# Filling the fourth 32 rows of the score operands with zeros, so that the score matmuls contract over all 128 rows

## The chip, the cores and the metric

The kernel runs on one core of one Trainium2 chip. The metric is the device time of one execution in microseconds (us). Every time below is of that one core.

## The reference

One block of a perceiver: cross attention from 256 queries to a context of 25088 rows, self attention over the 256 rows, and a feed-forward net, each with a residual. The change touches only the cross attention, whose scores go through a sigmoid and not a softmax:

```python
E, H, D = 512, 16, 32
q = (layernorm(x) @ Wq.T).reshape(B, L, H, D) * D ** -0.5      # L = 256
k = (ctx @ Wk.T).reshape(B, -1, H, D)                          # 25088 rows
v = (ctx @ Wv.T).reshape(B, -1, H, D)
scores = sigmoid(einsum('blhd,bshd->bhls', q, k))
o = einsum('bhls,bshd->blhd', scores, v).reshape(B, L, E)
x = x + o @ Wo.T
x = x + self_attention(layernorm(x))
x = x + ffn(layernorm(x))                                      # hidden width 2048
```

## The kernel before

The context is worked through in 49 chunks of 512 rows. The first chunk, then 22 turns of a loop over two chunks (`odd`, then `even`), then four more chunks written out. Float32 products are made from rounded parts: each operand is split into a high part and a rest (type float32r), and three of the four products of parts are added (`TERMS`).

Keys (line 748) and values (line 773) of a chunk are each made by a scheme of seven products of half-size blocks, `keys(1)` to `keys(7)` and `values(1)` to `values(7)`. One such product is 12 matmuls over 128 rows with 256 columns each. The vector and scalar engines add the products up, and the keys' high part and rest are copied by DMA into the key stack `kst`: for each head the 32 rows of the high part go to rows 0 to 31 of the stack, the rest to rows 32 to 63, and the high part once more to rows 64 to 95. The query stack `qst` holds the high part of the queries in rows 0 to 31, the same high part in rows 32 to 63, and the rest in rows 64 to 95. So one matmul over 96 rows gives all three products of a head of 32. Rows 96 to 127 of both stacks are not used by the scores before the change.

A score unit (line 789) is four such matmuls, one for each head of a group of four heads, against 128 context rows. It is written into one of two score tiles `sc`, and ScalarE takes the sigmoid of the whole unit (line 376) into `probs`. A chunk has 16 units. The weighing with the values (line 809) has four matmuls per unit, each over 128 rows, which write 32 rows of the sum `acc` side by side.

The order of TensorE's work is written out by hand. Mostly a pair of units (8 matmuls) is followed by a key product (12) and a value product (12). An entry into scores is a place where TensorE comes to line 789 from another line. The functions of the order give 8 entries in the first chunk, 9 in each of the next 46 (`odd` or `even`), 13 in chunk 47 (with the pairs of chunk 48 that it does ahead) and 3 in chunk 48: 8 + 46 * 9 + 13 + 3 = 438 entries with 784 units in all. Of these, 7 per chunk in 48 chunks, 336, are followed at once by key matmuls.

Several tiles lie on the same memory at different times. The second half of `kst` (`spare`) first holds sums of weights (`wk_sum`) and the transposed input (`xnT`), which the weight rounding and the query projection (line 870, semaphore `q_made`) read. Small unused tiles (`gap`) shift the addresses of some of the operands.

Of the kernel before, what the change touches and what calls it, by code (L numbers as in the profile page):

```python
# [21 lines left out]
P = 128  # L22
# [4 lines left out]
D = E // H  # L27
# [16 lines left out]
def f32(ap):  # L44
    return ap.bitcast(F32)
# [60 lines left out]
def cross_attention(nc, x, ctxT, wqT, wkT, wvT, woT, wqk, wv, bv, wo, w_all, biases, keep):  # L106
# [4 lines left out]
    ident, x1, qst, next_weights = keep["ident"], keep["x1"], keep["rows"][0], keep["weights"][1]  # L111
    with ExitStack() as stack:
# [3 lines left out]
        def sem(name):  # L116
            return stack.enter_context(nc.semaphore(name))
# [15 lines left out]
        kst, kst_f32 = keep["two_types"](stack, "k_stack", [P, 2, 2, HG, 2, HS])  # L133
# [40 lines left out]
        ident_zero, const_ready, chain = sem("ident_zero"), sem("const_ready"), sem("dve_chain")  # L174
        var_ready, sd_ready, xn_ready = sem("var_ready"), sem("sd_ready"), sem("xn_ready")
        xnT_made, xnT_ready, q_made = sem("xnT_made"), sem("xnT_ready"), sem("q_made")
        one_ready, zeros_ready = sem("one_ready"), sem("zeros_ready")
        xn1_ready, xn1T_made, xn1T_ready = sem("xn1_ready"), sem("xn1T_made"), sem("xn1T_ready")
        bv_loaded, v1_made, v1_ready = sem("bv_loaded"), sem("v1_made"), sem("v1_ready")
        q_hi, q_lo, q_stacked = sem("q_hi"), sem("q_lo"), sem("q_stacked")  # L180
        wk_summed, wv_summed = sem("wk_summed"), sem("wv_summed")
        wk_hi, wv_hi, wk_ready, wv_ready = sem("wk_hi"), sem("wv_hi"), sem("wk_ready"), sem("wv_ready")
# [164 lines left out]
        @block.gpsimd  # L347
        def _(pool):
            nc.gpsimd.memset(keep["one"][:, 0:1], 1.0).then_inc(one_ready, 1)
            nc.gpsimd.memset(zeros[:], 0.0).then_inc(zeros_ready, 1)  # L350
            nc.gpsimd.memset(bits[:], 0).then_inc(piece_used, 1)
            nc.gpsimd.memset(ident[:], 0.0).then_inc(ident_zero, 1)
            pool.wait_ge(ident_zero, 1)
            nc.gpsimd.affine_select(out=ident[:], in_=ident[:], compare_op=ALU.not_equal, fill=1.0,
                                    base=0, pattern=[[-1, P]], channel_multiplier=1).then_inc(const_ready, 1)

        @block.scalar
        def _(act):
# [354 lines left out]
        def _(pe):  # L713
# [66 lines left out]
            def scores(c, n, order, free):  # L780
                t, g = order[n]
                if free:
                    pe.wait_ge(probs_ready, c * (TC * G) + (n - 1))
                if t % 2 == 0 and g % 2 == 0:
                    q = {(0, 0): 0, (0, 2): 1, (2, 2): 2, (2, 0): 3}[t, g]
                    pe.wait_ge(lo_moved[q], c * MOVED + MOVED)
                    pe.wait_ge(hi_twice[q], c * 16 + 16)
                for j in range(HG):
                    last = nc.tensor.matmul(sc[g % 2][:, j * L:(j + 1) * L],  # L789
                                            kst[0:3 * D, t // 2, g // 2, j, g % 2, t % 2 * P:(t % 2 + 1) * P],  # L790
                                            qst[0:3 * D, j, g, :], start=True, stop=True)
                last.then_inc(scores_ready, 1)

            def weigh(c, par, units, order, first=False):
# [81 lines left out]
            for ready in (wk_ready, wv_ready):  # L876
                pe.wait_ge(ready, 8)
            pe.wait_ge(q_stacked, 3 * MOVED)

            def one(c, par, first, k_next, split_next, looped):  # L880
                m = c + 1
# [3 lines left out]
                def unit(n):  # L885
                    scores(c, n, order, not (first and n < 2))
# [19 lines left out]
                def last_pair(p):  # L906

                    scores(m, 2 * p, order, True)
                    scores(m, 2 * p + 1, order, True)
# [141 lines left out]
            for a, to in enumerate((kp, vp)):  # L1051
                for n, g in enumerate(GROUPS_DONE):
                    if a == 1 and n == G - 1:
# [3 lines left out]
                                            start=n == 0, stop=n == G - 1)  # L1057
# [513 lines left out]
def build(nc, x, ctxT, wqT, wkT, wvT, woT, wqk, bqk, wv, bv, wn, bn, wo, bo,  # L1571
          w_all, s1, s2, sh1, sh2, s3, out):
    with ExitStack() as stack:
# [6 lines left out]
        def two_types(stack, name, shape):  # L1580

            with nc.sbuf_tensor(f"{name}_r", shape, F32R) as as_f32r:
# [14 lines left out]
        keep |= {"wn": sb("wn_sb", [P, KE, H]), "bqk": sb("bqk_sb", [P, 2 * KE]),  # L1597
                 "bn": sb("bn_sb", [H, 1]), "bias_loaded": sem("bias_ld")}
        cross_attention(nc, x, ctxT, wqT, wkT, wvT, woT, wqk, wv, bv, wo, w_all, (wn, bqk, bn), keep)
        keep |= {"any_inexact": sb("any_inexact", [1, 1], mybir.dt.int32), "inexact_ready": sem("any_inexact_ready"),  # L1600
                 "x2": sb("x2", [P, LT, E]), "raw": sb("w_raw", [P, RING, UNIT]),
# [53 lines left out]
```

## Time and profile before

| | |
|---|---|
| Time, median of 3 runs | 1924.5 us (1924.48 to 1924.76) |
| Span of the profiled execution | 1916.8 us |
| Outside the span, by the median | 7.7 us |
| PE busy | 1903.9 us, 99% |
| DVE, ACT busy | 1201.8 us, 1014.5 us |
| POOL busy | 4.3 us |
| Granted TensorE clock | 1.00 from the first stretch to the last |

The profile page gives no separate device time for the profiled execution, only its span. The time of the kernel is therefore compared as its median, and the 7.7 us between span and median are what lies around the span. PE stands for TensorE's matmuls, PEld for its weight loads, DVE for the vector engine, ACT for the scalar engine, POOL for GpSimd. A matmul's own duration overlaps that of the next; how fast they follow each other is read from the starts of two groups and the number of matmuls between them.

### The profile page before, as it was taken

The page shows a single profiled execution, that of the slowest core. Times are in us where ns is not written, and L with a number is a line of the kernel's source. Part 1 is how long each engine was busy: PE and PEld are TensorE (multiplying, and loading weights), DVE is VectorE, ACT ScalarE, POOL GpSimd, SP SyncE. Part 2 cuts the span into 40 slices and gives each one's busy share as a digit, 9 for nine tenths or more (in the row PEclk, how much of TensorE's full clock was granted, in tenths as well). Part 3 has the DMA queues.
Part 4 walks back from the last instruction along what each step waited for, and adds up shares of the span by engine and source line. Part 5 has one row for each costly group of instructions (what it writes and reads, how often), then busy time and mean ns, then how long its engine had stood idle before and what let it go on. Part 6 is the DMA issues. An engine that isn't in the chain of part 4 may idle for free. (4 is left out here: it accounts for less than half of the span.)

```text
span 1916.8 us, 50813 instructions
## 1 busy us (share of the span) xinstructions
PE 1903.9 (99%) x19361; PEld 1708.7 (89%) x19362; DVE 1201.8 (63%) x2113; ACT 1014.5 (53%) x1132; POOL 4.3 (0%) x16
## 2 busy tenths in 40 slices
PE   9999999999999999999999999999999999999999
PEld 7989999999898999999889999999989999867998
DVE  7566676667667576666766766676676775436322
ACT  5455455555544555455554555545455454634864
POOL 0000000000000000000000000000000000000000
PEclk9999999999999999999999999999999999999999
DMA  7556555565656656566565565656556555454784
GB/s 212 149 154 169 142 153 159 155 157 142 167 147 156 169 132 157 154 159 156 152 167 144 149 166 140 166 140 162 150 156 165 141 153 128 108 219 147 279 303 165
DMA packets 128396, 310.92 MB, mean 162 GB/s; under 512 B 33889, under 2 KB 33889, under 8 KB 109665
## 3 DMA queue, kind: packets, MB, share of 16 engines
q1 hardware_dynamic: 95952, 214.10, 43.7%
q10 hardware_dynamic: 32400, 96.22, 15.9%
q8 instruction: 30, 0.49, 0.1%
q14 instruction: 14, 0.11, 0.0%
HBM read 153.95 MB, written 0.52 MB: 81 GB/s over the span
## 5 line engine op out<-in xcount | busy, mean ns | idle before, releaser
L376 ACT ACTIVATE probs<-sc 128x1024 f32<-128x1024 f32 x784 | 769.8, 1025 | 730.6 <-PE sc L789 594.9
L748 PE MATMUL kp<-x_combos,weights_r 128*128 128x256 f32 x4032 | 536.0, 280 | 0.0
L748 PEld LDWEIGHTS kp<-x_combos,weights_r 128*128 128x128 f32 x4032 | 491.5, 188 | 28.7 <-issue 28.4
L773 PE MATMUL vp<-more_weights,x_combos 128*128 128x256 f32 x4032 | 515.7, 277 | 0.0
L773 PEld LDWEIGHTS vp<-more_weights,x_combos 128*128 128x128 f32 x4032 | 485.3, 188 | 0.6 <-issue 0.4
L789 PE MATMUL sc<-rows_r,k_stack_r 96*128 96x256 f32 x3136 | 436.6, 280 | 0.1
L789 PEld LDWEIGHTS sc<-rows_r,k_stack_r 96*128 96x128 f32 x3136 | 396.3, 189 | 2.8 <-issue 1.6
L583 DVE TENSOR_TENSOR parts<-parts,kp 128x512 f32<-128x512 f32 x240 | 164.4, 685 | 325.7 <-PE kp L748 325.7
L809 PE MATMUL acc<-probs,v 128*32 128x256 f32 x6272 | 354.4, 380 | 0.0
L809 PEld LDWEIGHTS acc<-probs,v 128*32 128x32 f32 x6272 | 196.4, 110 | 131.0
L520 DVE TENSOR_TENSOR x_combos<-ctx_raw,x_combos 128x512 fp32r<-128x512 f32 x240 | 166.2, 692 | 8.2
L608 DVE TENSOR_TENSOR v<-parts,vp 128x512 f32<-128x512 f32 x144 | 98.8, 686 | 60.9 <-PE vp L773 60.9
L614 DVE TENSOR_TENSOR bits<-bits,weights 128x512 int32<-128x512 int32 x176 | 121.3, 689 | 24.1 <-DMA weights<-w_all_dram 20.2
L533 DVE CAST x_combos<-ctx_raw 128x512 fp32r<-128x512 f32 x240 | 101.2, 422 | 4.6 <-DMA ctx_raw<-ctxT_dram 0.8
L603 DVE TENSOR_TENSOR k_rows_lo<-parts,k_rows_hi 128x512 fp32r<-128x512 f32 x144 | 98.6, 685 | 0.1
L608 DVE TENSOR_TENSOR v<-v,vp 128x512 f32<-128x512 f32 x96 | 66.1, 688 | 44.0 <-PE vp L773 41.5
L1425 ACT ACTIVATE w_hi<-w_raw 128x2048 fp32r<-128x2048 f32 x42 | 80.2, 1911 | 0.0
L596 DVE CAST k_rows_hi<-parts 128x512 fp32r<-128x512 f32 x144 | 61.5, 427 | 26.3 <-DMA k_stack_r<-k_rows_lo 15.3
L520 DVE TENSOR_TENSOR x_combos<-x_sum,x_combos 128x512 fp32r<-128x512 f32 x96 | 66.5, 692 | 3.3
L577 DVE TENSOR_TENSOR k_rows_lo<-kp,k_rows_hi 128x512 fp32r<-128x512 f32 x48 | 33.0, 687 | 49.0 <-ACT k_rows_hi L390 48.9
L1541 PE MATMUL ps<-weights_r,w_hi 128*128 128x256 f32 x512 | 58.2, 277 | 0.0
L1541 PEld LDWEIGHTS ps<-weights_r,w_hi 128*128 128x128 f32 x512 | 58.1, 188 | 0.0
(159 smaller groups left out, 852.8 us busy)
## 6 DMA issues: line engine op xcount, KB each, us to landing
k_stack_r<-k_rows_hi SPq DMA_DIRECT2D x784, 64.0 KB, 2.3
k_stack_r<-k_rows_lo SPq DMA_DIRECT2D x784, 64.0 KB, 2.3
k_stack_r<-k_stack_r SPq DMA_DIRECT2D x196, 256.0 KB, 3.0
ctx_raw<-ctxT_dram ACTq DMA_DIRECT2D x47, 1024.0 KB, 6.4
weights<-w_all_dram ACTq DMA_DIRECT2D x176, 256.0 KB, 3.6
w_raw<-w_all_dram SPq DMA_DIRECT2D x44, 1024.0 KB, 4.8
weights<-wqk_dram SPq DMA_DIRECT2D x2, 1024.0 KB, 11.7
probs<-wkT_dram SPq DMA_DIRECT2D x2, 512.0 KB, 5.3
```

Source lines behind the costliest of these rows:

```text
L376: nc.scalar.activation(probs[:, place(par, n), :], sc[g % 2][:], ACT.Sigmoid).then_inc(probs_ready, 1)
L520: nc.vector.tensor_tensor(xc[:, i - 1, :, 1, :], x_source(raw, i), f32(xc[:, i - 1, :, 0, :]), ALU.subtract).then_inc(x_ready, 1)
L533: nc.vector.tensor_copy(xc[:, i - 1, :, 0, :], x_source(raw, i)).then_inc(x_hi, 1)
L583: nc.vector.tensor_tensor(to, kc[:, K_PART[add], :, :], k2, ALU.add).then_inc(k_sum, 1)
L603: nc.vector.tensor_tensor(kr_lo[:, at, :, :], to, f32(kr_hi[:, at, :, :]), ALU.subtract).then_inc(k_lo, 1)
L608: nc.vector.tensor_tensor(v_at(par, q), vt[:] if add == "t" else v_at(par, add), v2, ALU.add).then_inc(v_sum, 1)
L614: nc.vector.tensor_tensor(bits[:], bits[:], piece[:, t % 2, :], ALU.bitwise_or).then_inc(piece_used, 1)
L748: last = nc.tensor.matmul(k2[:, r, :], wk[i - 1][:, k, a, r * P:(r + 1) * P], xc[:, i - 1, k, b, :], start=i in FRESH and r == 0 and n == ...
L773: last = nc.tensor.matmul(v2[:, r, :], xc[:, i - 1, k, b, r * P:(r + 1) * P], wv_c[i - 1][:, k, a, :], start=i in FRESH and r == 0 and n == 0,
L789: last = nc.tensor.matmul(sc[g % 2][:, j * L:(j + 1) * L], kst[0:3 * D, t // 2, g // 2, j, g % 2, t % 2 * P:(t % 2 + 1) * P], qst[0:3 * D, ...
L809: last = nc.tensor.matmul(acc[D * j:D * (j + 1), g, :], v[:, par, t, h * D:(h + 1) * D], probs[:, place(par, n), j * L:(j + 1) * L], start ...
L1541: last = nc.tensor.matmul(ps[q][:, 0, :], wt[:, k, :], x[:, k, :], start=m == 0, stop=m == passes * KH - 1)
```

## The change

Before the first scores are made, GpSimd writes zeros into rows 96 to 127 of the query stack and of both halves of the key stack, 4096 float32 elements per row each. The memset of the second half waits for the two uses of `spare` that came before it. The score matmuls then name all 128 rows of both stacks. Zeros in both operands add nothing to the sums. TensorE waits for the three memsets once, ahead of the first scores.

```diff
+        q_rows_zero, k_rows_zero = sem("q_rows_zero"), [sem(f"k_rows_zero{i}") for i in range(2)]
...
             nc.gpsimd.affine_select(out=ident[:], in_=ident[:], compare_op=ALU.not_equal, fill=1.0,
                                     base=0, pattern=[[-1, P]], channel_multiplier=1).then_inc(const_ready, 1)
+            pool.wait_ge(const_ready, 1)
+            nc.gpsimd.memset(f32(qst[3 * D:P, :, :, :]), 0.0).then_inc(q_rows_zero, 1)
+            pool.wait_ge(q_rows_zero, 1)
+            nc.gpsimd.memset(f32(kst[3 * D:P, 0, :, :, :, :]), 0.0).then_inc(k_rows_zero[0], 1)
+            pool.wait_ge(wk_ready, 8)
+            pool.wait_ge(q_made, 1)
+            pool.wait_ge(k_rows_zero[0], 1)
+            nc.gpsimd.memset(f32(kst[3 * D:P, 1, :, :, :, :]), 0.0).then_inc(k_rows_zero[1], 1)
...
                     last = nc.tensor.matmul(sc[g % 2][:, j * L:(j + 1) * L],
-                                            kst[0:3 * D, t // 2, g // 2, j, g % 2, t % 2 * P:(t % 2 + 1) * P],
-                                            qst[0:3 * D, j, g, :], start=True, stop=True)
+                                            kst[:, t // 2, g // 2, j, g % 2, t % 2 * P:(t % 2 + 1) * P],
+                                            qst[:, j, g, :], start=True, stop=True)
...
             pe.wait_ge(q_stacked, 3 * MOVED)
+            pe.wait_ge(q_rows_zero, 1)
+            for zero in k_rows_zero:
+                pe.wait_ge(zero, 1)
```

## Rows read from the trace of the kernel before

**Rows 1.** The page: busy time, and the granted clock in 40 slices.
```profile
PE 1903.9 (99%) x19361; PEld 1708.7 (89%) x19362; DVE 1201.8 (63%) x2113; ACT 1014.5 (53%) x1132; POOL 4.3 (0%) x16
...
PEclk9999999999999999999999999999999999999999
```

**Rows 2.** The page's costliest groups: busy us, mean ns of one, idle before.
```profile
L789 PE MATMUL sc<-rows_r,k_stack_r 96*128 96x256 f32 x3136 | 436.6, 280 | 0.1
```

**Rows 3.** Timeline of PE, 866 to 916 us: start, duration, line, count.
```profile
900.04 1.09 PE L789 MATMUL sc<-rows_r,k_stack_r 96*128 96x256 f32 x8
...
903.70 1.09 PE L789 MATMUL sc<-rows_r,k_stack_r 96*128 96x256 f32 x8
904.62 1.53 PE L748 MATMUL kp<-x_combos,weights_r 128*128 128x256 f32 x12
905.99 1.52 PE L773 MATMUL vp<-more_weights,x_combos 128*128 128x256 f32 x12
907.35 1.09 PE L789 MATMUL sc<-rows_r,k_stack_r 96*128 96x256 f32 x8
...
911.00 0.63 PE L789 MATMUL sc<-rows_r,k_stack_r 96*128 96x256 f32 x4
```

**Rows 4.** The chain that ended last, the feed-forward net's stretch.
```profile
1782.07 116.05 PE ps L1541 x1024
```

**Rows 5.** Timeline of PE, 30 to 64 us, after the first weighing.
```profile
60.72 1.58 PE L748 MATMUL kp<-x_combos,weights_r 128*128 128x256 f32 x12
62.13 1.57 PE L773 MATMUL vp<-more_weights,x_combos 128*128 128x256 f32 x12
63.54 0.63 PE L789 MATMUL sc<-rows_r,k_stack_r 96*128 96x256 f32 x4
```

**Rows 6.** Timeline of PE, 866 to 916 us, after a weighing in the loop.
```profile
869.57 0.98 PE L748 MATMUL kp<-x_combos,weights_r 128*128 128x256 f32 x6
870.38 0.63 PE L789 MATMUL sc<-rows_r,k_stack_r 96*128 96x256 f32 x4
870.85 0.85 PE L748 MATMUL kp<-x_combos,weights_r 128*128 128x256 f32 x6
871.54 1.52 PE L773 MATMUL vp<-more_weights,x_combos 128*128 128x256 f32 x12
```

**Rows 7.** The same timeline, the last pair and value product of a chunk.
```profile
885.70 1.11 PE L789 MATMUL sc<-rows_r,k_stack_r 96*128 96x256 f32 x8
886.64 1.58 PE L773 MATMUL vp<-more_weights,x_combos 128*128 128x256 f32 x12
888.15 4.52 PE L809 MATMUL acc<-probs,v 128*32 128x256 f32 x80
```

**Rows 8.** Timeline of PE, 10 to 16 us: all 128 rows, different source tiles.
```profile
12.64 1.59 PE L836 MATMUL sc<-x_combos,v_r 128*128 128x256 f32 x12
14.08 1.52 PE L836 MATMUL sc<-x_combos,weights_r 128*128 128x256 f32 x12
15.44 0.73 PE L853 MATMUL vp<-more_weights,x_combos 128*128 128x256 f32 x5
```

**Rows 9.** Lines 789 and 748 by source: duration ns, minimum/median/maximum.
```profile
L789 PEld LDWEIGHTS sc<-rows_r,k_stack_r x3136: 186/188/193, 41.3 to 1690.3; 96*128 96x128 f32 x196
...
L748 PEld LDWEIGHTS kp<-x_combos,weights_r x4032: 186/188/194, 42.2 to 1663.6; 128*128 128x128 f32 x192
```

**Rows 10.** Timeline of POOL: the nearest memset, and its last work before 1711 us.
```profile
1.30 0.52 POOL L351 MEMSET bits<- 128x512 int32 x1
...
2.19 0.29 POOL L354 TENSOR_SCALAR_AFFINE_SELECT ident<-ident 128x128 f32<-128x128 f32 x1 [0.23 <-POOL ident L352]
```

**Rows 11.** Timeline, 0 to 45 us: an early DVE step, the query projection, the first scores.
```profile
6.66 0.69 DVE L561 TENSOR_TENSOR x_combos<-ctx_raw,x_combos 128x512 fp32r<-128x512 f32 x1 [0.55 <-ACT x_combos L414]
...
22.64 7.07 PE L870 MATMUL sc<-k_stack,probs 128*128 128x256 f32 x32
...
41.37 1.09 PE L789 MATMUL sc<-rows_r,k_stack_r 96*128 96x256 f32 x8
```

## The prediction

> **What bounds the kernel now.** I began with the page. TensorE is busy 99% of the span, and the clock is granted in full in all 40 slices [rows 1]. So the time moves only if TensorE's matmuls follow each other faster or slower, or are fewer; the change leaves their number alone. The costliest groups name the touched one: 3136 score matmuls with 0.1 us of idle time before them in all [rows 2]. Nothing is waited for there, so the remaining question is the spacing of matmuls inside an unbroken stream. For that I read the timeline of TensorE and divided the distance of two groups' starts by the matmuls between them.
>
> The feed-forward net gives the yardstick, a long stream over 128 rows: 1024 matmuls of 256 columns in 116.05 us, 113.3 ns each [rows 4]. In the chunk loop a cycle of 8 score, 12 key and 12 value matmuls takes 3.653 us (three cycles from 900.04 to 911.00 us) [rows 3]. At 113.3 ns the 32 would take 3.627 us, so 0.026 us are lost per cycle. The parts tell where: the values take 1.36 us, the yardstick's 12 * 113.3 = 1.360; the keys after scores 1.37, 0.010 more; the scores 0.92 to 0.93, about 0.016 over 8 * 113.3 = 0.907 [rows 3]. The going from keys to values, both over 128 rows, shows no loss at this resolution; going into and out of the 96-row scores does. The reader is to see that the loss sits exactly at the two borders where the row count changes.
>
> **What the change removes, adds and moves.** It removes nothing but, perhaps, those two losses. Entry into scores: 438 times 0.016 us is 7.0 us. Keys right behind scores: 336 times 0.010 is 3.4 us. Together 10.4 us; the rows are rounded to 0.01 us, so each of the two factors may be off by 0.003, some 2 us in the sum. I take 10. The bounds of this unknown price are 0 (the row count is not what costs there) and the full 10.4 us with what hangs on it. What may hang on it is the last pair and value product of a chunk: 8 scores in 0.94 and 12 values in 1.51 us ahead of the weighing [rows 7]. The going into the weighing costs its own 0.1 us (the four scores from 911.00 are followed by line 809 as well, and that switch stays). So scores and values there are some 0.02 and 0.05 us above the undisturbed cycle; if the spacing there came back too, 48 chunks would give another 3.4 us. That is the low end and not in the sum.
>
> The matmul itself: the same 256 columns stream through, and the weight load has the same 128 columns. The load's median is 188 ns over 96 rows and 188 ns over 128 rows [rows 9], so nothing is charged per matmul.
>
> Of the same matter the Trainium skill says (TensorE: Matmul & The Clock Gate, LDWEIGHTS) that a load's time goes by the columns and not by the contraction rows. The trace agrees for the load alone, 188 against 188 ns [rows 9]. By that rule alone the change would do nothing and the time would be 1924.5 us; the row loss of 0.026 us per cycle is what it does not speak of, and it is the second case below.
>
> What is added: three memsets on GpSimd of 4096 elements per row over 32 rows. The nearest row is 512 elements of 4 bytes in 0.52 us [rows 10]; eight times that is 4.2 us, an upper bound as it counts the fixed part eight times. GpSimd is free from 2.5 us on [rows 10], so the first two end by 11 us. The third waits for the query projection, which starts at 22.64 and ends at about 29.7 us [rows 11], and ends by 34. The first scores start at 41.37 us [rows 11]: 7 us of cover, and TensorE's new waits cost nothing. Without this cover each memset would cost its 4 us once. Nobody else waits for GpSimd until long after. What could suffer is DVE, which runs two-input operations such as that at 6.66 us [rows 11], during the second memset, and whose results TensorE awaits in the first 12 us. No row shows GpSimd and DVE at once. Bounds: 0, or such an operation doubled (0.69 us) at the two places where the first products wait for it, 1.4 us. I take 0, since TensorE idles for other arrivals in that stretch anyway. No DMA, queue or address is changed.
>
> The sum is 1916.8 - 10 = 1906.8 us of span; with the 7.7 us around it 1914.5 us, which is also the median less 10.
>
> **The rivals.** *The row count is not the cause (same).* Then the small losses come from what also changes at the border: source tiles and banks. For it: in the first stage, all over 128 rows, 12 matmuls with weights from `v_r` take 1.44 us (120 ns each) and the next 12 from `weights_r` 1.36 us (113.3) [rows 8]. So tiles alone can set the spacing. Against it: keys to values changes both tiles too and shows no loss. Time: 1924.5 us, between 1924 and 1926 with the start-up bound.
>
> *The slow spacing stays (slower).* After the first weighing, the stream runs at 1.41 us for 12 matmuls, 117.5 ns each: keys from 60.72 and values from 62.13 us [rows 5]. It does so over an unbroken 24 matmuls of 128 rows. In the loop the six keys behind a weighing take 0.81 us, then four scores follow, and the six keys after those take 0.69 us, 115 ns with the border loss in them, and the values behind them 1.36 or so a product [rows 3, 6]. So the slow spacing, once there, ends at an entry into scores, and in the rows of the loop I find it ending nowhere else. If it is the change of row count that resets it, 128-row scores reset nothing. Price: 0.05 us per product, 14 products in each of 48 chunks, of which some 70 are slow already, leaves 600 products or 30 us; the scores at 0.94 instead of 0.923 per pair add 0.02 * 390 = 8 us. The losses at the borders are contained in these figures, so the time would be 1924.5 + 38 = 1962.5 us with the slow spacing everywhere, and about 1943 with it in half of the stream. Against a gain of 10 us it decides from about 10 / 48, one fifth of the products. Against this rival: the feed-forward net keeps 113.3 ns over 1024 matmuls without any change of rows [rows 4], and the products of the first stage went from 120 to 113.3 ns with none either [rows 8]. So a reset exists that needs no 96 rows.
>
> *DVE or TensorE is held up at the start (slower).* 1.4 us as worked out, under 0.2%: it takes no share of its own.
>
> The waits for the zeros are no rival: they would have to be 7 us later than their bound.
>
> **How the numbers follow.** The border loss goes: 0.42, at 1914.5 us, its own range 1910 to 1919 (with the last pair's 3.4 us below, and with half of the loss left above). Nothing moves: 0.33, at 1924.5. The slow spacing stays in at least a fifth of the stream: 0.25, 1930 to 1963. The prediction is the likeliest, 1914.5 us. The range takes in the first two wholly and about half of the third: 1910 to 1943; left out are about 0.03 below and 0.12 above. Within 0.2% is within 3.8 us of 1924.5, about what a measurement of this kernel can tell from no change. Faster 0.42, same 0.33, slower 0.25.
>
> **What would show it.** In the timeline of the changed kernel the undisturbed cycle should take 3.63 us instead of 3.653: scores 0.91, keys 1.36. If it is still 3.65, the row count was not the cause. If after a weighing the second half of the keys and the values behind it take 0.705 and 1.41 us instead of 0.69 and 1.36, the slow spacing has outlived the scores, and the prediction is wrong on its sign. On POOL, three memsets of 3.5 to 4.2 us should end before 11 and 34 us, and the first scores start at 41.4 us; a start later by over 0.5 us would be the start-up cost. The clock should stay at 1.00.

## The result, and the profile after

The changed kernel takes 1935.23 us (median of 6 runs, 1931.97 to 1938.00) against 1924.51 us before (6 runs); the ratio is 1.0073 with a 95% interval of [1.0058, 1.0087]. It is slower, where a faster kernel, at 1914.5 us, was forecast.

The single times stand on two levels in both kernels, some 5.7 us apart: 1918.85 (once) and 1924.5 us before, 1932.35 and 1938.0 us after (medians of each level). Level against level the change costs 13.4 to 13.5 us. What makes the levels is found below. The profile before was of a run on the lower level (1916.8 us of span), that after too (1931.97 us, span 1930.3: 1.7 us lie around it).

The page after, first its busy times and the clock:

```profile
PE 1917.2 (99%) x19362; PEld 1721.5 (89%) x19362; DVE 1201.7 (62%) x2113; ACT 1016.6 (53%) x1132; POOL 14.8 (1%) x19
...
PEclk9999999999999999999999999999999999999999
...
L757 PE MATMUL kp<-x_combos,weights_r 128*128 128x256 f32 x4032 | 541.7, 280 | 0.0
...
L782 PE MATMUL vp<-more_weights,x_combos 128*128 128x256 f32 x4032 | 522.3, 278 | 0.0
...
L798 PE MATMUL sc<-rows_r,k_stack_r 128*128 128x256 f32 x3136 | 436.6, 279 | 0.1
```

Lines have moved by 9 from the keys on: 757, 782 and 798 are the keys, values and scores. The scores' group has the same busy time as before, 436.6 us [rows 2], although it alone was edited. The page before had 536.0 us for the keys and 515.7 for the values:

```profile
L748 PE MATMUL kp<-x_combos,weights_r 128*128 128x256 f32 x4032 | 536.0, 280 | 0.0
L773 PE MATMUL vp<-more_weights,x_combos 128*128 128x256 f32 x4032 | 515.7, 277 | 0.0
```

They took on 5.7 and 6.6 us. (Busy time counts overlapping matmuls once. From start to start of the groups, the scores take 369.8 us before and 370.0 after, the keys 6.1 us more, the values 6.9.) TensorE still waits for nothing; it is its spacing that changed.

The timeline of TensorE in the same stretch (start, duration, line, count) shows how:

```profile
886.88 1.08 PE L798 MATMUL sc<-rows_r,k_stack_r 128*128 128x256 f32 x8
887.79 1.53 PE L757 MATMUL kp<-x_combos,weights_r 128*128 128x256 f32 x12
889.15 1.52 PE L782 MATMUL vp<-more_weights,x_combos 128*128 128x256 f32 x12
890.52 1.11 PE L798 MATMUL sc<-rows_r,k_stack_r 128*128 128x256 f32 x8
...
904.47 1.58 PE L757 MATMUL kp<-x_combos,weights_r 128*128 128x256 f32 x12
905.88 1.57 PE L782 MATMUL vp<-more_weights,x_combos 128*128 128x256 f32 x12
907.29 1.08 PE L798 MATMUL sc<-rows_r,k_stack_r 128*128 128x256 f32 x8
908.21 1.52 PE L757 MATMUL kp<-x_combos,weights_r 128*128 128x256 f32 x12
909.57 1.52 PE L782 MATMUL vp<-more_weights,x_combos 128*128 128x256 f32 x12
910.93 1.11 PE L798 MATMUL sc<-rows_r,k_stack_r 128*128 128x256 f32 x8
911.87 1.58 PE L757 MATMUL kp<-x_combos,weights_r 128*128 128x256 f32 x12
913.29 1.57 PE L782 MATMUL vp<-more_weights,x_combos 128*128 128x256 f32 x12
914.70 1.08 PE L798 MATMUL sc<-rows_r,k_stack_r 128*128 128x256 f32 x8
```

Read the distances of starts. The cycle at 907.29 takes 3.64 us: scores 0.92, keys and values 1.36 each. The next, at 910.93, takes 3.77: 0.94, 1.42, 1.41. So cycles at 113.8 and at 117.8 ns per matmul stand side by side, where before the cycles of this kind took 3.65 us [rows 3]. Over the whole loop, by the matmuls' starts, there are 190 such cycles of 8, 12 and 12: before, 184 of them take 3.65 or 3.66 us; after, 94 take 3.64 and 96 take 3.76 or 3.77. An entry into scores mostly turns the spacing over: of the 168 entries from fast values or keys, 167 led to slow scores, and of the 263 from slow ones, 212 led to fast scores; the other 51 stayed slow. Before, of the 281 entries from fast values, 257 ended at the fast spacing; 23 of the other 24 are single units ahead of a weighing, too short to show the way back.

The start-up and the rest of the kernel are as forecast:

```profile
2.55 3.51 POOL L358 MEMSET rows_r<- 32x4096 f32 x1
6.12 3.51 POOL L360 MEMSET k_stack_r<- 32x4096 f32 x1
29.70 3.52 POOL L364 MEMSET k_stack_r<- 32x4096 f32 x1 [20.08 <-PE sc L879]
```
```profile
41.47 1.08 PE L798 MATMUL sc<-rows_r,k_stack_r 128*128 128x256 f32 x8
```

The memsets of the first fence (timeline of POOL) end at 6.1, 9.6 and 33.2 us, and the first scores (timeline of PE) start at 41.47, 0.1 us later than before [rows 11]. From there to the first matmul of the output projection, which I call the loop below, the kernel before takes 1652.0 us and the changed one 1665.25. These 13.2 us are the whole difference. The loop's time comes out of one profile to a few tenths (four profiles whose loop does the same work give 1652.0 to 1652.3 us) and does not hold the two levels, so the experiments are read by it first.

### The profile page after: what moved, and what is told of

The parts are those of the page before. It is cut to its first block and busy times, and to the rows that moved or that the text cites. A ratio compares the mean times of both kernels' runs of the same rounds, so it can differ in the third digit from the quotient of the medians.

```text
span 1930.3 us, 50820 instructions
## 1 busy us (share of the span) xinstructions
PE 1917.2 (99%) x19362; PEld 1721.5 (89%) x19362; DVE 1201.7 (62%) x2113; ACT 1016.6 (53%) x1132; POOL 14.8 (1%) x19
## 5 line engine op out<-in xcount | busy, mean ns | idle before, releaser
L385 ACT ACTIVATE probs<-sc 128x1024 f32<-128x1024 f32 x784 | 769.4, 1024 | 739.0 <-PE sc L798 604.3
L757 PE MATMUL kp<-x_combos,weights_r 128*128 128x256 f32 x4032 | 541.7, 280 | 0.0
L757 PEld LDWEIGHTS kp<-x_combos,weights_r 128*128 128x128 f32 x4032 | 497.2, 188 | 28.7 <-issue 28.4
L782 PE MATMUL vp<-more_weights,x_combos 128*128 128x256 f32 x4032 | 522.3, 278 | 0.0
L782 PEld LDWEIGHTS vp<-more_weights,x_combos 128*128 128x128 f32 x4032 | 491.0, 188 | 0.6 <-issue 0.4
L798 PE MATMUL sc<-rows_r,k_stack_r 128*128 128x256 f32 x3136 | 436.6, 279 | 0.1
L798 PEld LDWEIGHTS sc<-rows_r,k_stack_r 128*128 128x128 f32 x3136 | 396.2, 188 | 2.8 <-issue 1.6
L586 DVE TENSOR_TENSOR k_rows_lo<-kp,k_rows_hi 128x512 fp32r<-128x512 f32 x48 | 33.2, 691 | 40.4 <-ACT k_rows_hi L399 40.2
```

What stands on the lines that cost most here:

```text
L385: nc.scalar.activation(probs[:, place(par, n), :], sc[g % 2][:], ACT.Sigmoid).then_inc(probs_ready, 1)
L757: last = nc.tensor.matmul(k2[:, r, :], wk[i - 1][:, k, a, r * P:(r + 1) * P], xc[:, i - 1, k, b, :], start=i in FRESH and r == 0 and n == ...
L782: last = nc.tensor.matmul(v2[:, r, :], xc[:, i - 1, k, b, r * P:(r + 1) * P], wv_c[i - 1][:, k, a, :], start=i in FRESH and r == 0 and n == 0,
L798: last = nc.tensor.matmul(sc[g % 2][:, j * L:(j + 1) * L], kst[:, t // 2, g // 2, j, g % 2, t % 2 * P:(t % 2 + 1) * P], qst[:, j, g, :], s ...
```

## The experiments

The first four ask whether it is the row count at all, and which matmuls need fewer rows.

**The memsets alone.** The changed kernel with the slices of the score matmuls as before:

```diff
-                                            kst[:, t // 2, g // 2, j, g % 2, t % 2 * P:(t % 2 + 1) * P],
-                                            qst[:, j, g, :], start=True, stop=True)
+                                            kst[0:3 * D, t // 2, g // 2, j, g % 2, t % 2 * P:(t % 2 + 1) * P],
+                                            qst[0:3 * D, j, g, :], start=True, stop=True)
```

> The three memsets and their waits stay, the score matmuls go back to 96 rows. Theory A (the row count of the score matmuls decides how a changed spacing goes on: with 96 rows it falls back to 113 ns within three or four matmuls, with 128 rows it lasts until the next entry into scores): about 1924.5 us, and in the timeline the cycle of 8 scores, 12 keys and 12 values takes 3.65 us throughout. Theory B (the memsets shift the start, and the stream falls into another rhythm by that alone): 1932 to 1938 us, with cycles of 3.63 and 3.77 us by turns.

Loop 1652.1 us, ratio 1.0001 [0.9986, 1.0016]. Zeros and waits cost nothing; Theory B is out. This profile is of a run on the upper level, 1924.42 us, and shows where the levels come from. The chain that ended last (start, duration, line) of the kernel before, in the execution of [rows 4], had 29.30 us for 256 matmuls and then 116.05 us for the 1024:

```profile
1752.77 29.30 PE ps L1526 x256
```

Here:

```profile
1752.81 30.41 PE ps L1538 x256
1783.22 120.60 PE ps L1553 x1024
```

120.60 us over 1024 is 117.8 ns. The whole feed-forward net, 1280 matmuls over 128 rows, runs at the slow spacing in this execution and at the fast one in the other. 4.6 us here and 1.1 in the stretch ahead of it are the 5.7 us between the levels. All 17 profiled executions with an unchanged net have one or the other, 116.05 or 116.06 us in nine and 120.60 or 120.61 in eight, and wherever the kernel's times stand on two levels, the first goes with the lower.

**Part of the unit at 96 rows.** The changed kernel, each with `rows` in place of the fixed slice, `kst[0:rows, ...]` and `qst[0:rows, ...]`:

```diff
                 for j in range(HG):
+                    rows = 3 * D if j == 0 else P          # first96
+                    rows = 3 * D if j == HG - 1 else P     # last96
+                    rows = 3 * D + 16                      # rows112
+                    rows = P - 1                           # rows127
+                    rows = 3 * D if n % 2 == 0 else P      # even96
+                    rows = 3 * D if n % 2 == 1 else P      # odd96
```
(one of these lines in each run)

> Only the first matmul of each score unit contracts over 96 rows, the other three over 128. If it is the change of row count at an entry that sets the spacing back (A1), one matmul of 96 rows is enough: 1915 to 1925 us. If the stream must stay at 96 rows while the spacing recovers, over three or four matmuls (A2): near the changed kernel, 1930 to 1938 us. Theory B: 1932 to 1938 us.

Loop 1674.4 us, ratio 1.0118 [1.0089, 1.0147]: slower than either kernel.

> Only the last matmul of each score unit contracts over 96 rows, the other three over 128. A1 (a change of row count sets the spacing back wherever it is): 1915 to 1925 us, the slow spacing of the first three matmuls of a unit ending at its fourth. A2 (several matmuls of 96 rows are needed): 1930 to 1938 us. Theory B: 1932 to 1938 us.

Loop 1679.5 us, ratio 1.0146 [1.0119, 1.0173]. Neither A1 nor A2 foresaw that mixing row counts inside a unit would be worse than 128 rows throughout.

> The score matmuls contract over 112 rows, so that the fourth group of 32 rows is used by half. If it matters that a fourth group of 32 rows is used at all: as with 128 rows, 1932 to 1938 us. If any row count under 128 keeps the fast spacing: about 1924.5 us. Between the two if each further row adds to it.

Loop 1652.3 us, ratio 1.0012 [0.9998, 1.0026]: as with 96 rows.

**One row less than all.**

> The score matmuls contract over 127 rows, one less than all. Theory F (only the full 128 rows let the slow spacing last through the scores and beyond): the chunk loop takes 1652 us as before, not 1665, and the whole 13 us less than the changed kernel. Theory G (it goes by the count, more rows being worse, and 112 was still below a threshold): 1655 to 1665 us of loop.

Loop 1652.7 us, ratio 0.9990 [0.9976, 1.0004]. Theory F's number came and G falls: 127 rows do what 96 do. That only the full 128 rows let the slow spacing last, as F says, falls with the run at one row count below. It is not the number of rows that costs.

**The units by turns.**

> Score units of even number contract over 96 rows, those of odd number over 128. A2 (the spacing recovers within three or four matmuls as long as these are of fewer than 128 rows): the first unit of a pair recovers as before; the second brings one more border of row counts inside each pair. If such a border itself costs spacing (as the runs with one odd matmul out of four suggest), a loop of 1665 to 1680 us; if only the recovery counts, near 1652 us.

Loop 1680.0 us, ratio 1.0146 [1.0119, 1.0172]. By the starts, the first unit of a pair came to the fast spacing, the border in the middle of the pair turned it to slow in all 307 pairs whose starts can be read, and the keys and values behind kept it. The number of borders alone is not what costs: odd96, below, has a border inside each pair as well and takes 15 us less.

**One row count throughout.** The kernel before, with `[0:3 * D, ...]` in both operands of the key and value products of the loop too, so that a quarter of each such product is left out:

```diff
-                            last = nc.tensor.matmul(k2[:, r, :], wk[i - 1][:, k, a, r * P:(r + 1) * P],
-                                                    xc[:, i - 1, k, b, :], start=i in FRESH and r == 0 and n == 0,
+                            last = nc.tensor.matmul(k2[:, r, :], wk[i - 1][0:3 * D, k, a, r * P:(r + 1) * P],
+                                                    xc[0:3 * D, i - 1, k, b, :], start=i in FRESH and r == 0 and n == 0,
```

> The kernel before with the key and value products of the loop cut to 96 rows too, so that a quarter of every such product is left out and the whole stream of scores, keys and values has one row count. Theory R (a border between 96 and 128 rows is what costs at an entry into scores and behind it): the losses of 16 and 10 ns vanish, 1642 us of loop or less against 1652. Theory T (what costs there is the change of tiles, whatever the rows): 1652 us as before, the cycle still at 3.65 us, or a little less if the slow stretches after a weighing recover sooner.

Loop 1665.4 us, ratio 1.0069 [1.0043, 1.0096], on the side that neither theory gave. Of its 190 undisturbed cycles 94 took 3.64 or 3.65 us and 95 took 3.76 or 3.77. The stretch of its timeline that answers to the changed kernel's:

```profile
866.87 1.11 PE L789 MATMUL sc<-rows_r,k_stack_r 96*128 96x256 f32 x8
867.81 1.58 PE L748 MATMUL kp<-x_combos,weights_r 96*128 96x256 f32 x12
869.22 1.57 PE L773 MATMUL vp<-more_weights,x_combos 96*128 96x256 f32 x12
870.63 1.08 PE L789 MATMUL sc<-rows_r,k_stack_r 96*128 96x256 f32 x8
```

In the changed kernel these four groups started at 866.83, 867.77, 869.19 and 870.60 us: 0.94, 1.42, 1.41 there and 0.94, 1.41, 1.41 here. The loops agree to 0.1 us. So 128 rows throughout and 96 rows throughout are the same; what the kernel before had, and the change took away, is that the scores' row count differs from that of the products around them.

**A border of row counts alone.** The feed-forward net keeps one spacing over its 1024 matmuls, whichever tiles they read: by the starts it turns nowhere, neither in the kernel before nor in memset_only. There, in line 1541 of the kernel before:

```diff
+                                    rows = P - 1 if m // 8 % 2 else P              # ff_borders
+                                    rows = P - (32 * q + m) // 8 % 3               # ff_three
-                                    last = nc.tensor.matmul(ps[q][:, 0, :], wt[:, k, :], x[:, k, :],
+                                    last = nc.tensor.matmul(ps[q][:, 0, :], wt[0:rows, k, :], x[0:rows, k, :],
```
(one of the two lines in each run)

> The kernel before; in the feed-forward net's two square layers the contraction goes by turns over 128 and 127 rows, every 8 matmuls, so that one row in a half of the terms is left out. Nothing else changes at these borders, neither tiles nor banks. If a border of row counts costs by itself: the 1024 matmuls of line 1541 take longer than 116.05 us, by 0.5 to 2 us for 10 ns at each of 128 borders, or by 4 us more where the slow spacing of 117.6 ns sets in. If it costs only together with a change of tiles: 116.05 us.

The stretch takes 119.03 us against 116.05, 2.98 more. The groups of PE in it by form (busy, mean ns of one, idle before):

```profile
L1542 PE MATMUL ps<-weights_r,w_hi 127*128 127x256 f32 x256 | 35.3, 281 | 0.0
L1542 PE MATMUL ps<-weights_r,w_hi 128*128 128x256 f32 x256 | 34.6, 277 | 0.0
```

281 is the mean of a matmul at the slow spacing, 277 at the fast one. Read alone, this would say that 127 rows are slow. The next run was made for that.

> The kernel before; in the square layers of the feed-forward net the contraction goes over 128, 127 and 126 rows by turns, every 8 matmuls, one or two rows of it left out. Toggle (each border of row counts turns fast into slow and slow into fast, whichever way it goes): stretches at 113, 118, 113, 118 ns, regardless of the row count. Direction (a fall brings the slow spacing, a rise the fast one): 128 rows at 113, both 127 and 126 at 118 ns, about 3.7 us on the 116.05 us. Position of the mode by the tiles alone: 116.05 us.

119.01 us, and by form:

```profile
L1542 PE MATMUL ps<-weights_r,w_hi 128*128 128x256 f32 x191 | 25.6, 279 | 0.0
L1542 PE MATMUL ps<-weights_r,w_hi 127*128 127x256 f32 x160 | 21.9, 279 | 0.0
L1542 PE MATMUL ps<-weights_r,w_hi 126*128 126x256 f32 x160 | 21.9, 279 | 0.0
```

All three have the same mean: each row count is fast half of the time. By the starts of the 8-matmul stretches (0.92 or 0.94 us each), the spacing turned over at all 120 borders of row counts and nowhere else, and at all 127 borders of the run before. This is Toggle as expected, and Direction falls. The two levels of time are gone with it: the 8 runs of ff_three lie between 1921.7 and 1923.3 us, those of ff_borders between 1921.8 and 1923.5.

**The place of the key stack.** The changed kernel, the stack moved within the same memory (32 floats here; 16 and 48 in the same way):

```diff
-        gap("before_k_stack", 48)
+        gap("before_k_stack", 16)
         kst, kst_f32 = keep["two_types"](stack, "k_stack", [P, 2, 2, HG, 2, HS])
+        gap("after_k_stack", 32)
```

> The changed kernel with 128 rows, the key stacks moved down by 32 floats (128 bytes) in every partition and all other tiles where they were. Theory H (where the operands lie in memory against each other decides the spacing at an entry into scores): the loop differs from 1665 us by more than 3 us, one way or the other, and the turns of fast and slow cycles change. Theory F (row count alone): 1665 us and the same turns.

Loop 1685.1 us, ratio 1.0152 [1.0130, 1.0174]. Nearly all cycles are slow now:

```profile
897.21 1.11 PE L799 MATMUL sc<-rows_r,k_stack_r 128*128 128x256 f32 x8
898.15 1.58 PE L758 MATMUL kp<-x_combos,weights_r 128*128 128x256 f32 x12
899.57 1.58 PE L783 MATMUL vp<-more_weights,x_combos 128*128 128x256 f32 x12
900.98 1.11 PE L799 MATMUL sc<-rows_r,k_stack_r 128*128 128x256 f32 x8
```

> 128 rows, key stacks moved down by 16 floats (64 bytes), all other tiles in place. Theory U (with one row count throughout, an entry into scores changes the spacing by where the operands lie; the row count itself costs nothing): the loop is another than 1665 and 1685 us or equals one of them, and there may be a place where all cycles are fast, a loop of 1637 to 1645 us. Theory V (128-row scores cannot be fast whatever the place): 1665 us or more.

Loop 1687.7 us, ratio 1.0179 [1.0127, 1.0231].

> 128 rows, key stacks moved down by 48 floats (192 bytes). Theory U: any of the levels so far or a faster one, 1637 to 1645 us of loop, if the place suits. Theory V: 1665 us or more.

Loop 1688.5 us, ratio 1.0184 [1.0129, 1.0239].

```diff
-        gap("before_k_stack", 48)
+        gap("before_k_stack", 64)        # up16
```

> 128 rows in the scores, the key stacks and all tiles allocated behind them moved up by 16 floats (64 bytes). Theory U (place and row count decide together, one place may suit 128 rows): any loop from 1637 to 1690 us. Theory V (128 rows cannot be fast at any place): 1665 us or more. No theory names the place beforehand.

Loop 1688.4 us, ratio 1.0167 [1.0124, 1.0209], as with the stack 48 floats lower: those two places are 64 floats, 256 bytes, apart. (No gap behind the stack makes up for the move in up16, so all tiles behind it moved too, and the two runs differ by more than the place of the stack.) No place tried suits 128 rows better than the first.

And the kernel before, 96 rows, with the same move by 32 floats:

> The kernel before with 96 rows, key stacks moved down by 32 floats, as in the 128-row run that took 1685 us of loop. If the two borders of row counts set the spacing back wherever the operands lie: 1652 us, as before. If the place counts with 96 rows as well: a loop longer by 5 to 30 us, so that the change was bad at this place only by the match of place and row count.

Loop 1684.7 us against 1652.0, ratio 1.0179 [1.0139, 1.0220]. At this place 96 and 128 rows take the same within 0.5 us. Theory H holds: place and borders act together, and the two borders around the scores do not set the spacing right wherever the operands lie. Between U and V the places don't decide: all four gave the 1665 us or more that V allows, and a fast place for 128 rows was not found. What speaks for U is that the row count made no difference at two places, here and in the run with 96 rows throughout.

**Which border.**

> Score units of even number contract over 128 rows, those of odd number over 96: the row count then falls in the middle of a pair and rises at the end of it, ahead of the keys. X1 (it is the rise to the products' 128 rows behind the scores that brings the fast spacing back, as long as several matmuls of fewer rows lie ahead of it): keys and values fast, a loop near 1652 us. X2 (it is the fall of the row count at the entry that undoes what the change of tiles does): keys and values slow in at least half of the cycles, 1665 us of loop or more.

Loop 1665.1 us, ratio 1.0054 [1.0034, 1.0074]: X2's number, but neither rule. By the starts, the border in the middle of the pair turned the spacing in all 307 pairs whose starts can be read, 192 times to fast and 115 times to slow. The border behind the pair, where the tiles change as well, turned it in none of the 262 exits to keys: 147 went on fast and 115 slow. X1 falls with those 115. So a cycle that is entered fast turns to slow at the entry, to fast in the middle, and goes on fast; one that is entered slow mostly turns to fast, then to slow, and goes on slow. The two turns cancel, and whole chunks run fast and whole chunks slow.

**One border on purpose.** The changed kernel with `rows = P if n == 15 else 3 * D`, and with `rows = P if n >= 14 else 3 * D`:

> 96 rows in all score units but the last of each chunk (the second of the last pair), which goes over 128. In the kernel before, this pair enters fast behind the keys, its second unit and the value product behind it run slow (0.94 and 1.51 us). A border of row counts at the middle of this pair, and none between it and the values, is one toggle put to where it is wanted: if borders toggle there as in the feed-forward net, the values run fast, 48 times 12 times 4.3 ns or 2.5 us less, a loop near 1649.5 us. If a toggle that coincides with a change of unit has no effect: 1652 us.

Loop 1650.7 us, 1.3 less than before. The last pair of a chunk and its values, which answer to [rows 7]:

```profile
885.36 1.12 PE L799 MATMUL sc<-rows_r,k_stack_r 96*128 96x256 f32 x8
886.32 1.52 PE L782 MATMUL vp<-more_weights,x_combos 128*128 128x256 f32 x12
887.77 4.52 PE L819 MATMUL acc<-probs,v 128*32 128x256 f32 x80
```

(The group of 8 is shown with the form of its first matmul; its last four go over 128 rows.) The values take 1.45 us instead of 1.51: fast. So it goes in 23 of the 48 chunks, all but one of them followed by a weighing, as this one is; in the others the values stayed slow. Its times are 1917.4 to 1917.7 and 1923.1 to 1923.6 us, those of the kernel before beside them 1918.6 to 1919.4 and 1924.5 to 1925.0: lower by 1.5 on the lower level and by 1.3 on the upper, by the medians. The ratio over both levels, 0.9991 [0.9975, 1.0006], can't tell it from 1.

> 96 rows in all score units but the last pair of each chunk, which goes over 128, the same as the keys ahead of it and the values behind it, so that this pair has no border of row counts at all. With one row count an entry into scores turned fast into slow in the changed kernel: the whole pair and the values behind it then run slow, 0.02 us per pair more than before, a loop of 1653 us. If the second unit's own turn (fast to slow in the kernel before) comes on top, the values run fast and the loop takes 1650 us.

Loop 1651.8 us, ratio 1.0000 [0.9986, 1.0015]. The values behind the pair stayed slow, as the first of its two cases says, but the scores cost nothing more. No kernel tried is faster than the one before beyond the interval of the measurement.

## Why the prediction was wrong

**Right:** that TensorE's spacing is all that counts; that each matmul and load costs the same over 96 and 128 rows (436.6 us of busy time for the scores in both, [rows 2]); that the memsets hide, their length (3.51 us against a bound of 4.2) and the start of the first scores; that memory, queues and the clock (0.999 to 1.00) stay out of it. The 7.7 us outside the span were a misreading: 1.7 us lie around it, and the rest is that the profiled run stood on the lower level. It changed the sum by nothing, since the sum was made as a difference.

**The step that failed** is the first term: "Entry into scores: 438 times 0.016 us" and "keys right behind scores: 336 times 0.010". The loss was really there, but it was put down to the border of row counts because it sat there, and the sum lets it go with the border. The entry into scores turns the spacing over with one row count as well (128 or 96 throughout, loop 1665.3 and 1665.4 us). With a second row count the scores were back at the fast spacing after three matmuls of the first unit. By the starts in the trace the next matmul came 120, 118 and 118 ns behind each of these three, and 113 behind the fourth: 17 ns over the fast spacing, the 0.016 us of the sum. In the changed kernel, where no border is left, entries from fast values begin alike (117, 119 and 118 ns on average) and then stay at 118. At this place of the operands the border went with the end of the loss and did not cause it. Only the smaller part of the term was in part as priced: behind fast scores the second key matmul starts 115 ns after the first, against 121 or 122 before, and the fast cycle takes 3.64 us and not 3.65. Instead of -10.4 us the term was +13.2.

**The rival that came true** is the second, at a third of its price. "The slow spacing stays" was priced at 38 us if it stays everywhere and 19 for half. It stayed in about half of the cycles (96 of 190), because a later entry into scores turns it back; the scores' own 8 us did not come (0.2 us from start to start). Keys and values took on 6.1 and 6.9 us. Its sign was right. Its mark, "If after a weighing the second half of the keys and the values behind it take 0.705 and 1.41 us", did not show at that place (from 877.77 us it was 0.68 and 1.37), but the 1.41 us stood in half of the cycles.

**What spoke against this rival misled.** "The feed-forward net keeps 113.3 ns over 1024 matmuls without any change of rows" was read as a sign that a stream of 128 rows finds back to the fast spacing. The net of the other level keeps 117.8 ns over the same 1024. A long stream keeps whichever spacing it has; the profile of one execution showed one of the two. And "a reset exists that needs no 96 rows", from 120 to 113.3 ns at a change of tiles [rows 8], was true, but a change of tiles can turn the spacing either way.

**Still open:** why there are two spacings, and what a border of row counts does where tiles change with it. Alone it turns the spacing over each time (247 of 247), and in the middle of a pair, where the score tile changes as well, it did so too (307 of 307 in odd96 and in even96 each). From scores to keys it did not: before, all 332 such exits with regular distances kept their spacing over a border, and after, 331 of 332 kept it without one. At the entry, counting turns does not give the result either: with a border both fast and slow values ended in fast scores before. And unit15_128 worked in one kind of chunk and not in the other. That the place of the key stack decides too is shown; by which bits of the address is not, beyond the one pair of places 256 bytes apart that agree.

## What to carry to other kernels

When TensorE is busy 99% of the time, compare the distances of matmuls' starts, not busy times: the same instructions stand at 113.3 or 117.8 ns, and 4% of the stream is at stake. A loss found at a border may have another cause, and the border may be what ends it; before removing it, make one run with the suspected difference taken away on both sides (96 rows everywhere would have told this one). An edit that does no work, such as padding operands to full height, is still an edit of the rhythm, and in a tuned kernel it should be tried together with the places of its operands.

## What the runs showed of the hardware

Two steady spacings exist for float32r matmuls of 256 columns with a weight load each: 113.3 ns (116.05 us for 1024) and 117.8 ns (120.60 us for 1024), at a granted clock of 1.00 in both. The Trainium skill (TensorE: Matmul & The Clock Gate, Wait — 56ns, not 53.3ns?) gives one spacing for matmuls back to back, the columns over 2.4 GHz and some 2.5 ns. For 256 columns that is an estimate of 109.2 ns, and no run here shows it: both spacings, with a weight load for each matmul, lie above.

A change of the number of contraction rows from one matmul to the next, by as little as one row (128 to 127, 127 to 126), turned the stream of the feed-forward net from one to the other, in either direction, within three or four matmuls, at 247 of 247 borders. Which of the counts it was did not matter there, nor did it matter in the loop whether all matmuls went over 96 or all over 128 rows (1665.4 and 1665.3 us). Between scores and keys, where the tiles change too, such a border turned nothing with the key stack at its first place (332 of 332 in the kernel before).

The place of an operand in memory changes the spacing as well: with the key stack 128 bytes lower the loop took 1685.1 us over 128 rows and 1684.7 over 96, against 1665.3 and 1652.0.

The same program falls into one or the other in its feed-forward net from execution to execution, which alone makes two levels of time 5.7 us, 0.3%, apart. A change smaller than that is to be read level by level or by a stretch of the trace.
